# Weight maxima and low parts placed elsewhere in the opening two steps of a gated attention and expert block, and one group of low probabilities moved to GpSimd

## The reference

```python
q = (layernorm(x) @ Wq + bq); k = (y @ Wk + bk); v = (y @ Wv + bv)      # 16 heads of 16
attn = softmax(q k^T / sqrt(16))
h = relu((attn v) @ W1 + b1);  x = x + tanh(g_xattn) * (h @ W2 + b2)    # W1 256x512, W2 512x256
z = layernorm(x)
p = softmax(max(z @ gate_W + gate_b, 1e-4))                              # 8 experts
comb = top-2 of max(p, 0.1), divided by their sum
out = x + tanh(g_ffn) * sum_e comb_e * (z @ expert_W[e] + expert_b[e]) / 2
```

## Time and profile before

| | us |
|---|---|
| median of 3 runs | 991.95 |
| the runs | 991.95, 992.25, 987.53 |
| profiled execution, time | 988.13 |
| profiled execution, span | 986.4 |
| PE busy | 931.3 |
| DVE busy | 854.7 |
| ACT busy | 720.2 |
| GpSimd busy | 642.4 |

### The profile page before, as it was taken

How to read it: one execution, slowest core, us unless ns; L and a number is a source line. 1 busy time by engine, 2 the same in 40 slices (tenths; PEclk the granted TensorE clock), 3 DMA queues, 4 the chain that set the end, 5 groups by cost and what they waited for, 6 DMA issues and landing times.

```text
span 986.4 us, 26160 instructions
## 1 busy us (share of the span) xinstructions
PE 931.3 (94%) x9410; PEld 670.0 (68%) x9410; DVE 854.7 (87%) x2139; ACT 720.2 (73%) x1517; POOL 642.4 (65%) x792
## 2 busy tenths in 40 slices
PE   3679999999999999999999999999999999999987
PEld 2557777767776776776677677667767677777763
DVE  5787888988989888898898889889888988988875
ACT  4756878777787877777787777778777778777661
POOL 5445666667776567776666777666677766667743
PEclk8579999999999999999999999999999999999999
DMA  6000000000000000000000000000000000000000
GB/s 199 27 15 11 15 15 26 26 25 22 26 15 15 25 26 25 24 15 25 15 25 25 25 23 15 25 15 27 25 26 22 16 14 26 25 12 12 13 12 22
DMA packets 17471, 24.61 MB, mean 25 GB/s; under 512 B 2798, under 2 KB 8896, under 8 KB 17344
## 3 DMA queue, kind: packets, MB, share of 16 engines
q1 hardware_dynamic: 17344, 22.94, 7.4%
HBM read 14.54 MB, written 8.39 MB: 23 GB/s over the span
## 4 chain that ended last, share of the span: by engine, by line
PE 78%; DVE 10%; ACT 5%; issue 5%; POOL 1%; DMA 0%; POOLq 0%; ACTq 0%; DVEq 0%
PE e L740 28%; PE g L740 18%; PE t L923 9%; PE t L789 4%; PE g L940 3%; PE s L874 3%; PE s L811 2%; PE s L810 2%; PE s L809 2%; DVE row_max L1256 2%; PE g L749 2%; ACT p_f L557 2%; DVE acc L1211 2%; DVE p_lo L1194 2%; ACT p_hi L558 2%
## 5 line engine op out<-in xcount | busy, mean ns | idle before, releaser
L373 POOL TENSOR_TENSOR p_lo<-p_f,p_hi 77x512 f16<-77x512 f32 x160 | 184.4, 1168 | 221.5 <-ACT p_hi L558 221.5
L740 PE MATMUL e<-we_hi,x2T_lo 128*128 128x512 f16 x496 | 188.5, 380 | 4.8 <-DVE acc L1211 4.6
L740 PE MATMUL e<-we_hi,x2T_hi 128*128 128x512 f16 x496 | 187.8, 379 | 0.0
L740 PE MATMUL e<-we_lo,x2T_hi 128*128 128x512 f16 x496 | 187.8, 379 | 0.0
L557 ACT ACTIVATE p_f<-t 77x512 f32<-77x512 f32 x256 | 152.6, 596 | 27.5 <-PE t L789 25.0
L1211 DVE SCALAR_TENSOR_TENSOR acc<-e,comb,acc 128x256 f32<-128x256 f32 x307 | 146.2, 476 | 13.8 <-PE e L740 11.5
L558 ACT ACTIVATE p_hi<-t 77x512 f16<-77x512 f32 x256 | 152.6, 596 | 0.0
L1256 DVE TENSOR_REDUCE row_max<-s 128x6 f32<-128x462 f32 (+1 forms) x192 | 108.6, 579 | 19.8 <-PE s L874 19.2
L809 PE MATMUL s<-v_hi,p_lo 77*128 77x17 f16 x1024 | 98.3, 172 | 9.1 <-DVE p_lo L1194 6.1
L809 PEld LDWEIGHTS s<-v_hi,p_lo 77*128 77x128 f16 x1024 | 84.0, 96 | 29.5 <-issue 10.6
L636 ACT ACTIVATE scaled<-e,comb 128x256 f32<-128x256 f32 x126 | 56.4, 475 | 65.2 <-PE e L740 65.2
(11 more groups left out here) (194 smaller groups left out, 2881.0 us busy)
## 6 DMA issues: line engine op xcount, KB each, us to landing
x_sb<-in_x SPq DMA_DIRECT2D x32, 256.0 KB, 2.6
out<-acc SPq DMA_DIRECT2D x32, 256.0 KB, 2.0
we_f<-in_L_ffn_expert_W SPq DMA_DIRECT2D x2, 1024.0 KB, 9.5
y_sb<-in_ctx SPq DMA_DIRECT2D x32, 57.8 KB
w_f<-in_L_xattn_W SPq DMA_DIRECT2D x2, 512.0 KB, 7.4
wq_f<-in_L_xattn_Wq SPq DMA_DIRECT2D x1, 256.0 KB, 4.1
wkv_f<-in_L_xattn_Wk SPq DMA_DIRECT2D x1, 192.0 KB, 2.9
wkv_f<-in_L_xattn_Wv SPq DMA_DIRECT2D x1, 192.0 KB, 3.9
```

Of the source, the lines that this page charges most:

```text
L373: pool.tensor_tensor(p_lo[:, r].rearrange("m h n -> m (h n)"), p_f[:, r, :], p_hi[:, r].rearrange("m h n -> m (h n)"), ALU.subtract).then_ ...
L740: mm = pe.matmul(out_ap, a, c, start=(first and i == 0), stop=(last and i == n - 1))
```

## The change

In step 0, DVE takes the maxima of half 0 of the expert weights where it took all before; `b2g_rows`, half 1, the gate weights, w1, the join and the powers come at the end of the step, behind the row maxima. PE's transpose of the maxima comes at the end of step 0, its spreading of the powers in step 1 behind the first two score groups. The scales are made in step 1 between `xnT_low` and `p_low(0, 0)`. ACT makes w1's high part, the experts', the gate's and the biases' in step 1 between the exponentials and ahead of `oT_high`; of the weights only w2 stays in step 0. DVE's low parts of w2, w1 and parts 0 to 2 of the experts go to places in step 1. PE's wait for the expert weights goes from the end of step 1 into step 2. `p_low(0, 7)`, of the first batch alone, is made by GpSimd behind its five other groups, and the counts that `attend` waits for follow that.

```diff
--- before.py
+++ after.py
@@ -49,6 +49,7 @@
 PARTS = 4
 POOL_LOW = (1, 3, 4, 5, 6)
 VECTOR_LOW = (0, 2, 7)
+FIRST_LOW = 7
 QUAD = 32
 SCALED = (2, 3)
 ADDED = [i for i in range(PAIRS) if i not in SCALED]
@@ -455,6 +456,8 @@
                 if has(s, -1):
                     for g in POOL_LOW:
                         p_low(m, g)
+                if has(s, -1) and m == 0:
+                    p_low(m, FIRST_LOW)
                 if has(s, 0):
                     key_blocks(b, 0)
                 if has(s, -2):
@@ -661,6 +664,9 @@
                     gate_tanh()
                 if mid:
                     exps(m, 2)
+                if s == 1:
+                    first_layer_high()
+                    experts_high((0,))
                 if first:
                     gate_exps(e)
                 if mid:
@@ -668,6 +674,8 @@
                     exps(m, 4)
                 if front:
                     k_high(b)
+                if s == 1:
+                    experts_high((1,))
                 if mid:
                     exps(m, 5)
                     exps(m, 6)
@@ -678,8 +686,9 @@
                     k_stack_high(b)
                 if s == 0:
                     weights_high()
-                    first_layer_high()
-                    experts_high((0, 1))
+                if s == 1:
+                    experts_high((2, 3))
+                    gate_and_biases_high()
                 if mid:
                     oT_high(m)
                 if first:
@@ -687,9 +696,6 @@
                     bias_copy(e, eu)
                 if front:
                     kz_copy(b)
-                if s == 0:
-                    experts_high((2, 3))
-                    gate_and_biases_high()
                 if mid:
                     relus(m, 0)
                     relus(m, 1)
@@ -795,10 +801,12 @@
                 if g == 0:
                     pe.wait_ge(v_split, 2 * b + 2)
                     pe.wait_ge(max_taken, 6 * b + 6)
-                if g in VECTOR_LOW:
-                    pe.wait_ge(p_lo_vector, len(VECTOR_LOW) * b + VECTOR_LOW.index(g) + 1)
+                if b == 0 and g == FIRST_LOW:
+                    pe.wait_ge(p_lo_pool, len(POOL_LOW) + 1)
+                elif g in VECTOR_LOW:
+                    pe.wait_ge(p_lo_vector, len(VECTOR_LOW) * b + VECTOR_LOW.index(g) + (0 if b else 1))
                 else:
-                    pe.wait_ge(p_lo_pool, len(POOL_LOW) * b + POOL_LOW.index(g) + 1)
+                    pe.wait_ge(p_lo_pool, len(POOL_LOW) * b + POOL_LOW.index(g) + (2 if b else 1))
                 r, half = g % RING, g // 4
                 for e in range(2):
                     h = 2 * g + e
@@ -982,12 +990,16 @@
                 if mid:
                     scores(m, 0)
                     scores(m, 1)
+                if s == 1:
+                    power_spread()
                 if s == B + 1:
                     gate_scores(e, eu)
                 if last and s <= B + 1:
                     experts(f, fu, 5, s - 3, (lambda: transposes_y(pair, b, u)) if front else None)
                 elif front:
                     transposes_y(pair, b, u)
+                if s == 2:
+                    experts_weights()
                 if first and s <= B:
                     gate_scores(e, eu)
                 if mid:
@@ -1026,12 +1038,8 @@
                     attend(m, mu, 7)
                 if first:
                     experts(e, eu, 0, s - 2)
-                if s == 0:
-                    largest_weight_transposed()
                 if front:
                     scores_for_max(b, 0)
-                if s == 0:
-                    power_spread()
                 if s == B + 1:
                     experts(e, eu, 1, s - 2)
                     experts(e, eu, 2, s - 2)
@@ -1076,12 +1084,12 @@
                 if front:
                     query_stack_transposes(b, 0)
                     query_stack_transposes(b, 1)
+                if s == 0:
+                    largest_weight_transposed()
                 if first and s <= B:
                     experts(e, eu, 4, s - 2)
                 if mid:
                     second_norm_transposes(m)
-                if s == 1:
-                    experts_weights()
 
             run(step)
 
@@ -1117,13 +1125,18 @@
                 dve.wait_ge(tanh_ready, 1)
                 dve.tensor_scalar(ffn_scale[:], tanh_g[:, 1:2], 1.0 / TOP_K, None, ALU.mult).then_inc(ffn_scale_ready, 1)
 
-            def weights_low():
+            def output_bias():
                 dve.wait_ge(w_loaded, 16 * WEIGHTS)
+                dve.wait_ge(tanh_ready, 1)
                 dve.tensor_scalar(b2g_rows[:], b2_rows[:], tanh_g[:, 0:1], None, ALU.mult).then_inc(b2g_ready, 1)
+
+            def second_layer_low():
+                dve.wait_ge(w_hi_ready, 3)
+                dve.tensor_tensor(w2_lo[:], w2_f[:], w2_hi[:].bitcast(F32), ALU.subtract).then_inc(w_lo_ready, 1)
+
+            def first_layer_low():
                 dve.wait_ge(w_scale_done, 1)
                 dve.tensor_scalar(b1_scaled[:], b1_cols[:], w_scale[:, 2:3], None, ALU.mult).then_inc(b1_scaled_ready, 1)
-                dve.wait_ge(w_hi_ready, 3)
-                dve.tensor_tensor(w2_lo[:], w2_f[:], w2_hi[:].bitcast(F32), ALU.subtract).then_inc(w_lo_ready, 1)
                 dve.wait_ge(w_hi_ready, 4)
                 dve.scalar_tensor_tensor(out=w1_lo[:], in0=w1_f[:], scalar=w_scale[:, 2:3], in1=w1_hi[:],
                                          op0=ALU.mult, op1=ALU.subtract).then_inc(w_lo_ready, 1)
@@ -1377,6 +1390,8 @@
                     key_value_weights_low()
                 if front:
                     xnT_low(b)
+                if s == 1:
+                    weight_scales()
                 if mid:
                     p_low(m, 0)
                 if front:
@@ -1391,6 +1406,8 @@
                     gate(e, eu, 2)
                     gate(e, eu, 3)
                     gate(e, eu, 4)
+                if s == 1:
+                    second_layer_low()
                 if mid:
                     p_low(m, 2)
                 if first:
@@ -1400,7 +1417,7 @@
                 if front:
                     kv_with_bias(b)
                 if s == 1:
-                    experts_low(1)
+                    first_layer_low()
                 if first:
                     gate(e, eu, 8)
                     gate(e, eu, 9)
@@ -1412,12 +1429,9 @@
                     q_high(b)
                 if s == 0:
                     largest_expert_weights(0)
-                    largest_expert_weights(1)
-                    largest_weights()
                     gate_factors()
-                    power_of_largest()
                 if s == 1:
-                    experts_low(2)
+                    experts_low(0)
                 if first:
                     gate(e, eu, 11)
                 if last:
@@ -1432,8 +1446,11 @@
                     add_expert(f_pair, f, fu, 6, 0, s - 3)
                 if last:
                     add_expert(f_pair, f, fu, 6, 1, s - 3)
-                if mid:
+                if s == 1:
+                    experts_low(1)
+                if mid and m > 0:
                     p_low(m, 7)
+                if mid:
                     reciprocals(m, 0)
                     normalise(m, 0, 0)
                     normalise(m, 0, 1)
@@ -1447,10 +1464,10 @@
                     take_max(b, 0)
                 if last:
                     add_expert(f_pair, f, fu, 7, 1, s - 3)
+                if s == 1:
+                    experts_low(2)
                 if mid:
                     oT_low(m)
-                if s == 0:
-                    weight_scales()
                 if front:
                     take_max(b, 1)
                 if has(s, 1) and s > 0:
@@ -1504,8 +1521,10 @@
                 if mid:
                     x2T_low(m, mu)
                 if s == 0:
-                    weights_low()
-                    experts_low(0)
+                    output_bias()
+                    largest_expert_weights(1)
+                    largest_weights()
+                    power_of_largest()
 
             run(step)
```

More of the change, by code:

```diff
@@ L1434, in step @@
                     add_expert(f_pair, f, fu, 6, 1, s - 3)
+                if s == 1:
+                    experts_low(1)
+                if mid and m > 0:
+                    p_low(m, 7)
                 if mid:
-                    p_low(m, 7)
                     reciprocals(m, 0)
```

## The result

The median of 8 runs is 983.53 us (980.75 to 984.14); the kernel before has 990.67 beside it (8 runs, 987.53 to 992.25). The ratio is 0.9930, 95% interval 0.9912 to 0.9948: faster, and the whole interval lies beyond the 0.5% that a measurement tells from no change. 7.1 us were gained where 5.5 were forecast. The profiled execution took 984.14 us with a span of 982.4, against 988.13 and 986.4.

What follows compares the result with a forecast made beforehand. TensorE (PE), busy 94% of the span, bounds the kernel; time can be won only where it idles, in the first 70 us. 5.4 - 0.2 + 0.3 = 5.5 us gives 982.6 or 986.4 by base; forecast 985.0, range 980.0 to 990.0.

Steps and rivals of the forecast that it cites:

- Step 0, gain 5.4: End of step 0: PE's two stalls shrink, x transposes start at 28.1 instead of 33.49; gain 5.4 us, bounds 4.6 to 6.4.
- Head of step 1, loss 0.2: Start of step 1: power_spread finds its input ready, four tiny scale instructions delay yT_low; loss 0.2 us (0 to 0.6).
- ACT in step 1, nothing: Step 1: ACT's moved high parts and copies fit idle stretches of 2.57, 1.45 and 4.92 us; no cost.
- rival 4: Step 0's time reappears in step 1; if half of ACT's work does not fit, 3.3 us lost: 988.3; chance 0.08.
- Middle of step 1, gain 0.3: Attention in step 1: p_low(0, 7) on GpSimd frees DVE, port collisions return most; gain 0.3 us, bounds -2.3 and +1.6.
- The two collisions named: Step 1's port: we_lo part 1 against GpSimd's low parts, and experts_low(2) ahead of oT_low, late 1.2 to 2.3 if shut out.
- Rival 1: Middle of step 1: we_lo's parts lose several port turns, -2.3 us instead of +0.3, giving 987.6; chance 0.15.
- Rival 2: Step 2: PE's clock granted 1.00 throughout, 28.8 us instead of 31.45, 2.6 more gained, 982.4; chance 0.15.
- Rival 3: Clock stays at 1.2 GHz through 58.1 to 68.3 and the next ten us; slower, 997.4; chance 0.04.
- two bases: Whole kernel: starting times for the forecast, profiled execution 988.13 and median 991.95 us; less 5.5, 982.6 and 986.4.
- three signs of being wrong: Step 1's xnT_hi off 29.2 by over 0.6; distance to step 2's not 35.0 to 35.6; next distance not 31.4.

Runs made afterwards that it cites:

- x5: Changed kernel with one semaphore increment, which does no work, added at the head of DVE's stream; 980.00 us.
- x3: Changed kernel with the maxima of the weights, their transpose and the scales back in their old places in step 0; 987.89 us.
- x7: x5 with PE's transpose of the maxima moved behind the x transposes of step 1; 979.29 us.
- x2: Kernel before with only p_low(0, 7) moved to GpSimd; 983.93 us.
- x10: Kernel before with one semaphore increment added at the head of DVE's stream; 986.70 us.
- x1: Changed kernel with p_low(0, 7) put back on DVE; 980.94 us.
- x8: x5 with we_lo parts kept clear of GpSimd's low parts and oT_lo, and ACT's last high part, gate and biases behind its kz copy; ratio 0.9901.
- x4: Changed kernel with ten unused matmuls added at the end of PE's step 1; step 2 took 31.43 us, total time not given.
- x6: Changed kernel with 128 semaphore increments added at the head of DVE's stream; 992.91 us.

## Why the prediction was right, and where it was not

**Step 0, gain 5.4: right in mechanism; the size holds once a later start is taken out.** L771 was to start at 27.7 and started at 28.78; the x transposes came at 28.95 instead of 28.1, and `xnT_hi` at 30.04 instead of 29.2. That is 0.8 us late, more than the 0.6 that the prediction allowed, and the gain between the profiles, 4.54 us at the x transposes, lies just under its lower bound of 4.6. The chain of waits of the kernel after has the reason ahead of all that the change touches:

```profile
17.99 2.48 POOL k_block L428 x2
```

The first key block came at 17.99, 1.11 us after that of the earlier trace rows: PE's query matmuls took 0.41 us each down to the last, at 15.18, where before they took 0.28 from 13.76 on. Counted from the first key block, the x transposes come 28.95 - 17.99 = 10.96 us later, and 33.49 - 16.88 = 16.61 before: a gain of 5.65, where the sum has 5.4. x5 has the same 10.96, x3 14.72, x7 10.42. The links held too: from the second row maximum to the stack transposes 4.09 us (4.10 in the sum), from b2g to the end of the join 3.94 (3.85). DVE's chain was last as forecast, though by 0.54 (10.96 less x7's 10.42) and not 1.1.

**Head of step 1, loss 0.2.** L775 and the scales lie beside other work, more than supposed: from `xnT_hi` to PE's first key and value matmul it takes 2.60 us after (30.04 to 32.64) and took 2.57 before (34.61 to 37.18). The loss is 0.03 us.

**ACT in step 1, nothing: right, which disposes of rival 4.** Timeline of ACT in step 1 after, against the earlier trace rows:

```profile
34.66 1.16 ACT L526 ACTIVATE we_hi<-we_f,w_scale 128x1024 f16<-128x1024 f32 x1
36.33 0.59 ACT L560 ACTIVATE p_f<-t 77x512 f32<-77x512 f32 x1 [0.51 <-PE t L795]
38.56 1.16 ACT L526 ACTIVATE we_hi<-we_f,w_scale 128x1024 f16<-128x1024 f32 x1
40.49 0.59 ACT L560 ACTIVATE p_f<-t 77x512 f32<-77x512 f32 x1 [0.77 <-PE t L795]
45.49 2.22 ACT L526 ACTIVATE we_hi<-we_f,w_scale 128x1024 f16<-128x1024 f32 x2
```

Behind the two single parts ACT still waits 0.51 and 0.77 us for PE's scores, and behind the pair, the gate and the biases 0.20 for the transposes of `oT`. What was to cost the copies' time was covered each time, by little.

**Middle of step 1, gain 0.3 with bounds -2.3 and +1.6: the place right, the distance 36.02 just outside 35.0 to 35.6.** From `xnT_hi` to the end of `oT_lo` it takes 20.95 us after and took 21.59 before, so 0.64 is gained where the sum had 0.3. The two collisions named came: among GpSimd's low parts (1.1 us, 1.0 of it for part 1), and part 2 ahead of `oT_lo` (0.7 us); GpSimd's `q_low` took 2.13 instead of 1.60.

The failed step is that nothing was set down behind `oT_lo`. From its end to the next `xnT_hi` it takes 15.07 us where it took 13.80, and the two traces show two causes for these 1.27. The first is the clock. Attention now ends while it is low: from 51.09 the MLP ran at 1.2 GHz for 2.9 us, until 54.0, before for 1.75. Its first twelve matmuls take 2.72 us against 2.32, a score chunk behind them 0.57 against 0.36, and ACT's last `h_f` ends 6.10 us behind `oT_lo` where it ended 5.52 behind it. The second is a third collision at the port, which that delay of 0.58 brings about. GpSimd's `x_with_bias` starts 5.7 to 5.8 us behind `oT_lo` in both kernels. DVE's fourth `h_lo` started ahead of it before; now it comes behind it and takes 1.11 us instead of 0.43 (two rows after, two rows before), and PE stands 0.80 us for it:

```profile
56.67 1.28 POOL L367 TENSOR_TENSOR xb<-x_sb,b2g_rows 128x512 f32<-128x512 f32 x1
57.12 1.11 DVE L1302 TENSOR_TENSOR h_lo<-h_f,h_hi 128x256 fp32r<-128x256 f32 x1 [0.30 <-ACT h_f L608]
...
61.75 0.43 DVE L1289 TENSOR_TENSOR h_lo<-h_f,h_hi 128x256 fp32r<-128x256 f32 x1 [0.31 <-ACT h_f L605]
61.98 1.35 POOL L366 TENSOR_TENSOR xb<-x_sb,b2g_rows 128x512 f32<-128x512 f32 x1
```

0.58 and 0.68 make 1.26. x2, whose clock was low there too, shows the same 1.11; in x5 `h_lo` takes 0.42, but the low clock lasts to 55.4, and the distance is 14.90. So step 1 as a whole is 0.6 us longer than before where 0.1 was to be gained.

Nor is the 35.39 before typical: x10, the same order of work, shows 36.42 and 32.39 for steps 1 and 2 in its profile, x5 35.64 and 32.29. From x10 to x5 the profiles give 5.3 in step 0, 0.8 in step 1 and 0.1 in step 2, and these 6.2 agree with the medians' 6.7.

By the prediction's reckoning a wait of one instruction at most would have made the middle worth 1.2. The rule of the Trainium skill, "SBUF — State Buffer", section "SBUF: two separate sides", is that whichever instruction starts first holds the pair for its own length. The runs are on both sides of it. `comb` in the steady steps waits for one instruction at most (1.17 us), as the rule says; p_low(0, 7) on DVE waited 4.12 us again in x1, through three instructions of GpSimd. The rule does not say who is next when both queue, and here GpSimd's queue went on.

**The rivals.** Rival 1's collisions came, 1.1 and 0.7 us, but did not outweigh what the stretch up to `oT_lo` won (step 1 as a whole lost 0.6 by the two profiles, not 2.3); the profile of x8 shows what they withheld, 1.9 us. Rival 2's condition (step 2 wholly at 1.00) was met in no run, and where the fall at its head was missing (x4, x5) a later stretch came and the step took 31.43 and 32.29 us. What decides when a late low stretch comes stays open. Rival 3's, a step 1 at 1.2 GHz throughout, did not come.

**The base.** The forecast lay between two bases, 988.13 and 991.95. The median of 8 turned out as 990.67; with the 5.5 this makes 985.2, and 983.53 is 1.7 below. Step 0 accounts for some 0.3 of this and step 1 for 0.7 (0.8 from x10 to x5, against the sum's 0.1). The rest was not found; single executions of the kernel before lie up to 4.7 us apart. Two of the prediction's three signs of being wrong came in the profile: `xnT_hi` of step 1 was 0.8 us late, and step 1 lasted 0.4 us beyond its range; step 2, 31.40, was as forecast. The profiled pair won 4.0 us where the medians won 7.1, and that 5.5 lies between the two is in part luck: steps 1 and 2 together differ by 2.0 us between the profiles of before and x10, whose order of work is the same, and no term of the sum holds that.

## What to carry to other kernels

Find the stretch in which the bounding engine idles, and put work that only releases later work behind what it waits for; a stall of 5.8 us went by changing the order alone. Work moved into idle time of an engine with a shared port has to be laid against the other engine's turns too, one piece at a time: here such pieces gave back 1.8 us of what freeing DVE had won. Whoever shifts a stage should look behind it as well: 0.6 us of delay moved one instruction to the wrong side of another engine's, which cost 0.7 more. And before small differences are explained, count the lengths of the steady steps in both traces: a step that is longer for no reason of its own can hide or feign more than the edit does.

## What the runs showed of the hardware

- At a place in DVE's stream that recurs every 128 recorded instructions (63, 703, 831, 2239 records ahead) an instruction started late: 0.41 us among bare increments (x6), 0.37 in the second norm (x2), 0.09 at `comb`. x2's step 8 lasted 28.79 us all the same; where it makes a two-input instruction miss its turn at the port it cost 1.7 us a step. One instruction more removed that, 128 more restored it.
- A DVE instruction that came 0.11 us ahead of the end of GpSimd's took the next turn; one that came some 0.02 ahead did not (both taken against the ends in the trace), and waited out the next one, 1.17 us instead of 0.23.
- Increments of a semaphore on DVE follow one another 0.092 to 0.093 us apart (x6). The 128 of them put DVE's first instruction off by 9.4 us and not by 12.3, because 2.9 us of them (0.82 to 3.71) fell into its wait for x.
- Kernels that differ by one semaphore increment show different low stretches of the clock in their first 90 us (before and x10, after and x5), and single executions of one kernel lie 4.7 us (before) and 7.5 us (x5) apart. Whether the one makes the other was not taken apart. Ahead of the first entry of the record (40.4 us after, 13.7 before) the view reads 1.00 while matmuls of 256 columns take 0.41 us, as they do at 0.50 later; there, the durations are to be believed.
